# Node features loaded already turned, normalised by VectorE with scales read back from memory, edges normalised by ScalarE: a graph network layer on one Trainium2 core

## The reference, cut to what matters

```python
h = relu(layernorm(x))                          # x: 50000 x 128, no gain or bias
rel_inputs = concat([h[src], h[dst], edge_attr], -1)       # 25000 edges, receivers = dst
rel_effects = relu(rel_inputs @ re_w1 + re_b1) @ re_w2 + re_b2     # hidden width 256, out 128
agg_effects = segment_sum(rel_effects, receivers, 50000)
out = x + relu(concat([h, agg_effects], -1) @ ea_w1 + ea_b1) @ ea_w2 + ea_b2
```

## Time and profile before

| | |
|---|---|
| median of three runs | 955.74 us |
| profiled execution | 956.01 us, of it span 954.1 us |
| PE busy | 97% of the span |
| DVE, ACT, POOL busy | 78%, 63%, 64% |
| mean granted TensorE clock | 0.987 of full speed |
| moved by DMA | 151.88 MB, mean 159 GB/s |

### The profile page before, as it was taken

The page is one execution under the profiler, slowest core; times in us unless marked ns, Lnnn a source line. Parts: engine busy times, 40 slices in busy tenths (PEclk is TensorE's granted clock), DMA queues, the critical chain, the costliest instruction groups (busy, mean ns, idle before and its releaser), DMA issues.

```text
span 954.1 us, 21049 instructions
## 1 busy us (share of the span) xinstructions
PE 923.3 (97%) x6450; PEld 817.8 (86%) x6450; DVE 740.1 (78%) x2155; ACT 605.5 (63%) x1180; POOL 609.1 (64%) x600
## 2 busy tenths in 40 slices
PE   4879999999999999999999999999999999999987
PEld 4668998898898899889889889988988988998876
DVE  5887788788788878878877887886887788788562
ACT  1447666666666766666666676666666667666653
POOL 7785776776677677677667767767766776772320
PEclk7979999999999999999999999999999999999999
DMA  6253655555565565555556556555555655554442
GB/s 200 75 148 113 183 163 168 150 177 175 151 186 168 151 183 163 168 151 176 172 155 185 167 153 183 162 169 158 169 174 151 186 167 152 169 177 146 124 123 76
DMA packets 114105, 151.88 MB, mean 159 GB/s; under 512 B 17984, under 2 KB 70080, under 8 KB 113984
## 3 DMA queue, kind: packets, MB, share of 16 engines
q1 hardware_dynamic: 101440, 124.73, 43.2%
q0 software_dynamic: 12544, 25.72, 10.2%
HBM read 104.92 MB, written 45.46 MB: 158 GB/s over the span
## 4 chain that ended last, share of the span: by engine, by line
PE 94%; DVE 3%; SPq 1%; issue 1%; ACT 1%; DMA 0%; DVEq 0%
PE l_ps L531 33%; PE l_ps L546 27%; PE l_ps L536 17%; PE agg_ps L496 7%; PE edge_ps L479 4%; PE node_ps L487 4%; PE node_ps L471 1%; SPq L294 0%; DVE rel_row L831 0%; DVE hot L844 0%; SPq L300 0%; DVE lo L804 0%; DVE h L797 0%; DMA drow_i<-in_dst_rows 0%; DMA win<-rel_rows 0%
## 5 line engine op out<-in xcount | busy, mean ns | idle before, releaser
L386 POOL DMA_INDIRECT gath<-in_x,dst_all x196 | 200.2, 1022 | 59.7 <-issue 59.7
L386 POOL DMA_INDIRECT gath<-in_x,src_all x196 | 195.0, 995 | 52.9 <-issue 51.7
L546 PE MATMUL l_ps<-w2n,hid 128*128 128x128 f32 x1568 | 193.6, 277 | 0.0
L655 ACT ACTIVATE hid<-l_ps,b1n 128x512 f32<-128x512 f32 x196 | 135.0, 689 | 82.4 <-PE l_ps L536 82.4
L409 POOL TENSOR_TENSOR ea_lo<-ea_in,ea_hi 128x512 fp32r<-128x512 f32 x45 | 74.3, 1651 | 171.6 <-ACT ea_hi L629 171.6
L546 PEld LDWEIGHTS l_ps<-w2n,hid 128*128 128x128 f32 x1568 | 182.9, 192 | 0.1
L810 DVE SCALAR_TENSOR_TENSOR lo<-node_ps,hi 128x512 fp32r<-128x512 f32 x98 | 67.3, 687 | 146.1 <-ACT hi L638 146.1
L663 ACT ACTIVATE h<-xin,shift,rs 128x128 f32<-128x128 f32 x392 | 165.2, 486 | 0.0
L531 PE MATMUL l_ps<-hi,w1n_hi 128*128 128x512 f32 x392 | 155.7, 397 | 0.4 <-ACT hid L655 0.4
L531 PE MATMUL l_ps<-hi,w1n_lo 128*128 128x512 f32 x392 | 155.4, 396 | 0.0
L402 POOL TENSOR_TENSOR xb<-xin,b2n 128x512 f32<-128x512 f32 x98 | 131.0, 1354 | 33.5 <-DVE res L838 33.5
(11 more groups left out here) (98 smaller groups left out, 1566.1 us busy)
## 6 DMA issues: line engine op xcount, KB each, us to landing
win<-rel_rows SPq DMA_DIRECT2D x392, 98.0 KB
xin<-in_x_tiles SPq DMA_DIRECT2D x98, 256.0 KB, 4.2
out<-res SPq DMA_DIRECT2D x98, 256.0 KB, 3.4
rel_rows<-rel_row SPq DMA_DIRECT2D x49, 392.0 KB, 2.4
ea_in<-in_ea_t SPq DMA_DIRECT2D x49, 256.0 KB, 3.2
gath<-in_x,src_all POOLq DMA_INDIRECT x196, 2.7
gath<-in_x,dst_all POOLq DMA_INDIRECT x196, 2.9
w1e<-in_L_gnn_re_w SPq DMA_DIRECT2D x1, 384.0 KB, 3.6
```

The source lines that it names most:

```text
L386: nc.gpsimd.indirect_dma_start(gath[b][:, s, k, :], None, x, bass.IndirectOffsetOnAxis(ap=idx[:, e * T + k:e * T + k + 1], axis=0)).then_i ...
L546: last = nc.tensor.matmul(l2_ps[turn % 2][:, k * P:(k + 1) * P], hid[r][:, c, k * P:(k + 1) * P], w[:, c, :], start=(c == 0), stop=(c == C ...
L655: nc.scalar.activation(hid[r][:, c, :], l1_ps[c][:, :], ACT.Relu, bias=b[:, c:c + 1]).then_inc(hid_set, 1)
```

## The change

The host hands over a second copy of x with features on partitions (`x_t`), and SP loads from it a 128 x 512 piece for each node tile (`load_xt`). `turn_nodes` and `node_ps` go; the freed bank gives each tile of a pair its own `agg_ps`. Statistics still come from `xin`. As nodes now lie along the free dimension, the scale and shift of each node are needed on all partitions: DVE writes them to `norm`, SP stores them to memory (`keep_norm`, 8 KB), waits for that, and loads them back to every partition (`load_norm`, 1 MB), a pair ahead of their use. DVE applies them with four operations of 128x512 a pair (`normalise_pair`), the high and low parts of features are taken from SBUF, and edges of joint steps are normalised by ACT in four portions between its `hidden` operations. The orders of all engines are rewritten: on SP the loads of `x_t` stand ahead of the windows; on POOL `keep_x` stands ahead of the gathers; on DVE `mark(2)` and all lows of features stand ahead of `edge_results`. `edge_step` keeps its edge normalisation on DVE.

```diff
+            def load_xt(r, j):
+                wait(sp, normed[r], j - 1)
+                sp.dma_start(xt[r][j % 2][:, :], columns(x_t, tile_no(r, j))).then_inc(xt_loaded[r][j % 2], 16)
+            def keep_norm(j, fast):
+                sp.wait_ge(shift_set, stats_turn(j, fast) + 1)
+                wait(sp, norm_loaded[j % 2], 16 * (j // 2))
+                sp.dma_start(node_norm[j % 2, :].rearrange("(p f) -> p f", p=P),
+                             norm[j % 2][:, 1, :, :].rearrange("p v f -> p (v f)")).then_inc(norm_kept, 16)
+            def load_norm(j):
+                sp.wait_ge(norm_kept, 16 * (j + 1))
+                for r in (1, 2):
+                    wait(sp, normed[r], j - 1)
+                sp.dma_start(spread_norm[j % 2][:, :, :, :, :].rearrange("p n v r k -> p (n v r k)"),
+                             node_norm[j % 2:j % 2 + 1, :].to_broadcast([P, P * ST])).then_inc(norm_loaded[j % 2], 16)
...
             def joint_step(e, j):                      (SP)
-                for r in (1, 2):
-                    if j + 1 < NJ:
-                        load_window(r, j + 1)
+                ahead = pair_of(e + 1)
+                for r in (1, 2):
+                    load_xt(r, j + 1)
+                for r in (1, 2):
+                    load_window(r, j + 1)
                 if e + 2 < EG:
                     load_ea(e + 2)
+                keep_norm(ahead, True)
                 if j > 0:
                     store(2, j - 1, True)
+                load_norm(ahead)
...
                 store_rel(e, True)
                 store(1, j, True)
...
             def joint_step(e, j):                      (POOL)
+                for r in (1, 2):
+                    keep_x(r, j + 1, True)
                 set_dst(e)
                 if e + 2 < EG:
                     gather(e + 2)
                 if e + 1 < EG:
                     low_ea(e + 1)
...
             def joint_step(e, j):                      (PE)
                 for r, n in ((0, e), (1, j), (2, j)):
                     for c in range(C):
                         layer1(r, n, turn + r, c)
-                if j + 1 < NJ:
-                    turn_nodes(1, j + 1)
-                    sum_window(1, j + 1)
+                sum_window(1, j + 1)
                 if e + 1 < EG:
                     turn_edges(e + 1)
                 layer2(0, turn)
                 layer2(1, turn + 1)
-                if j + 1 < NJ:
-                    turn_nodes(2, j + 1)
-                    sum_window(2, j + 1)
+                sum_window(2, j + 1)
                 layer2(2, turn + 2)
...
             def joint_step(e, j):                      (ACT)
                 if more:
-                    normalise(1, j + 1, True)
+                    high_ea(e + 1, True)
                 hidden(0, turn, 0, before_edge(e, True))
...
                 hidden(0, turn, 1, before_edge(e, True))
                 if more:
+                    normalise_edges(e + 1, range(0, 1))
                 hidden(1, turn + 1, 0, before_node(1, j, True))
+                if more:
+                    normalise_edges(e + 1, range(1, 2))
                 hidden(1, turn + 1, 1, before_node(1, j, True))
...
+                high_features(1, j + 1, True)
+                high_features(2, j + 1, True)
+                high_sums(1, j + 1, True)
                 if more:
                     high_edges(e + 1)
                 edge_highs(e, True)
                 edge_mids(e)
+                high_sums(2, j + 1, True)
...
+            def scale_nodes(r, j):
+                dve.wait_ge(norm_loaded[j % 2], 16 * (j // 2 + 1))
+                dve.wait_ge(xt_loaded[r][j % 2], 16 * (j // 2 + 1))
+                wait(dve, node_lo_set, tile_no(r, j - 1) + 1 if j > 0 else 0)
+                nc.vector.tensor_tensor(tiled(h[r]), tiled(xt[r][j % 2]), norm_of(0, r, j), ALU.mult).then_inc(scaled[r], 1)
+            def shift_nodes(r, j):
+                dve.wait_ge(scaled[r], j + 1)
+                nc.vector.tensor_tensor(tiled(h[r]), tiled(h[r]), norm_of(1, r, j), ALU.add).then_inc(normed[r], 1)
...
             def joint_step(e, j):                      (DVE)
...
                 if j > 0:
                     node_results(2, j - 1, True)
                 invert(*what)
-                if e + 1 < EG:
-                    normalise_edges(e + 1, range(T))
-                if more:
-                    mark(1, j + 1)
-                    low_nodes(1, j + 1)
+                mark(1, j + 1)
+                normalise_pair(j + 1)
+                mark(2, j + 1)
+                low_features(1, j + 1)
+                low_features(2, j + 1)
+                low_sums(1, j + 1)
                 if e + 1 < EG:
                     low_edges(e + 1)
                 edge_results(e, True)
-                if more:
-                    mark(2, j + 1)
                 edge_rests(e)
                 node_results(1, j, True)
                 edge_lows(e)
-                if more:
-                    low_nodes(2, j + 1)
+                low_sums(2, j + 1)
```

More of the change, by code:

```diff
@@ L99, in gnn_program @@
         rest = sb("rest", [P, T, D])
-        tiles = [2 * T, T, T]
         parts = [2, 2, 2]
-        h = [sb(f"h{r}", [P, tiles[r], D]) for r in range(3)]
+        h = [sb("h0", [P, 2 * T, D]), sb("h1", [P, G]), sb("h2", [P, G])]
         st = sb("st", [P, ST, 6])
@@ L110, in gnn_program @@
         sd = sb("sd", [P, ST])
-        rs = [sb(f"rs{b}", [P, ST]) for b in range(2)]
-        shift = [sb(f"shift{b}", [P, ST]) for b in range(2)]
+        norm = [sb(f"norm{b}", [P, 2, 2, 2 * T]) for b in range(2)]
+        spread_norm = [sb(f"spread_norm{b}", [P, P, 2, 2, T]) for b in range(2)]
         hi = [sb(f"hi{r}", [P, parts[r], G], F32R) for r in range(3)]
@@ L119, in gnn_program @@
         xb = [None] + [[sb(f"xb{r}{b}", [P, T, D]) for b in range(2)] for r in (1, 2)]
+        xt = [None] + [[sb(f"xt{r}{b}", [P, G]) for b in range(2)] for r in (1, 2)]
         win = [None] + [sb(f"win{r}", [P, T, ROW]) for r in (1, 2)]
@@ L161, in gnn_program @@
         normed = [sem(f"normed{r}") for r in range(3)]
+        norm_kept = sem("norm_kept")
+        norm_loaded = [sem(f"norm_loaded{b}") for b in range(2)]
+        scaled = [None] + [sem(f"scaled{r}") for r in (1, 2)]
         edges_turned = sem("edges_turned")
@@ L455, in joint_step @@
                     low_ea(e + 1)
-                if j + 1 < NJ:
-                    for r in (1, 2):
-                        keep_x(r, j + 1, True)
             def pair_step(j, fast):
@@ L578, in enter @@
                 pe.wait_ge(loaded[1], LOADS)
-                for r in (1, 2):
-                    turn_nodes(r, 0)
-                    (sum_window if fast else sum_windows)(r, 0)
+                if not fast:
+                    for r in (1, 2):
+                        sum_windows(r, 0)
             def joint_step(e, j):
```

212 lines of the change are left out of this document (114 added, 98 removed).

## The result

| | before | after |
|---|---|---|
| median | 955.92 us (954.33 to 956.46) | 1120.97 us (1116.97 to 1124.07) |
| ratio | | 1.173 (95%: 1.170 to 1.176) |
| span of the profiled execution | 954.1 us | 1122.3 us |
| first and last store of edge results in the joint steps | 86.20, 910.97 us | 93.09, 1073.89 us |
| mean step, store to store (45) | 18.33 us | 21.80 us |

The changed kernel is 17% slower. Slower was forecast; the predicted 1053 us was 68 us too low, and the time lies 6 us above the range (1022 to 1115).

The account below looks back on a forecast made before the run. PE's work was taken to bound the kernel at 18.34 us a step; the change closes a 20.5 us loop through SP. 45 x (20.5 - 18.34) = +97, beginning -1.5, tail +2: span 1051.6, time 1053 us, range 1022 to 1115.

Parts of the forecast that it names:

- the loop through SP: Joint step: edge store, second tile's window loads, landing, `mark(2)`, `edge_results`, `edge_lows`, store; 20.5 us against 18.34; chance 0.70.
- The rival that PE stays the bound: Second tile's windows on SP land within 10.3 us of the store, all turning is won: 916 us; chance 0.09.
- The 40 us of turnings: PE's turning matmuls (line 487) go, 40 us over the span, leaving PE a step of 17.45 us.
- the beginning: Before the first joint step: loses two turnings and some order, about -1.5 us.
- the tail: After the joint steps: two of the three pair steps each carry the new SP issues, +2 us.
- The lock: Rival: `keep_x(1)` on POOL holds DVE's `edge_lows` for 0.6 to 1.2 us; 1107 to 1121 with half rate; chance 0.15.
- The node operations: DVE's four 128x512 scale and shift operations a step, 0.69 us each, next starting after 0.61: 2.4 us a step.
- the near row: Strided reads of scales and shifts on DVE cost 0.2 us an operation, 0.8 in all, covered; taken as nothing.
- The cover of 1.3 us: DVE free at 12.1 us after the store, windows land at 13.4; norm arithmetic free unless dearer than 0.9 us each.
- The landing: From SP's last window issue to data and semaphore for the mark: 1.8 us; extra bytes may add 0 to 0.5.
- The clock: Rival: gaps in PE's step make its granted clock fall in each step: 1150 us; chance 0.04.
- POOL's loop: `keep_x` ahead of gathers, waiting for `node_results(2)`: 1.3, 10.6 for eight gathers, 2.4 landing: 14.3 us, inside 20.5 less statistics.

Follow-up runs that it names:

- the experiment meant for it: Changed kernel with scales read from adjacent elements, plus POOL's gathers ahead of both `keep_x`: 1123.61 us, ratio 1.177.
- the fastest reordered kernel: Changed kernel, DVE, SP and POOL reordered, each portion of ACT's edge normalisation moved behind the `hidden` operation it stood ahead of: 1025.40 us, ratio 1.075.
- the first reordered kernel: Changed kernel with turned features behind x, `mark(1)` behind node operations, `mark(2)` behind `edge_results`, POOL's order `low_ea`, gathers, `keep_x` twice: 1076.27 us, ratio 1.122.
- the second: As the first reordered kernel, but POOL's order is gathers, `low_ea`, `keep_x` twice: 1098.17 us, ratio 1.149.

## Why the prediction was right or wrong

**What bounds the kernel, and the direction.** PE's work stopped being the bound, and the loop through SP took over: shown by the kernel before with only its mark moved (+31 us), by the chain, and by the measured terms, of which SP's to the last issue (11.56 against 11.6) and DVE's from the mark to `edge_results` (3.63 against 3.62) came out. What was wrong is a rival that belonged into the sum and terms that were too small. The rival that PE stays the bound fell: it needed the second tile's windows within 10.3 us of the store, and they were issued, not yet landed, at 11.56. The 40 us of turnings were taken from PE, but its busy time in the joint steps did not fall: 18.33 us a step before, 18.62 after (18.5 in the steps at full granted clock), where I had 17.45 left. The share of 0.85 that I had forecast (17.45 of 20.5) came out as 18.62 of 21.80, which is luck.

**Where the 71 us of span beyond the forecast went.** The joint steps took 980.8 us against 922, +59; the beginning +8.4 (93.09 instead of 86.20 less 1.5); the tail +3.3 (48.4 after the last store, forecast 45.1).

**The lock was a rival and should have been a term.** Of the 59 us, 45 x 0.88 = 40 are the stretch from `edge_results` to `edge_lows`. I gave this rival 0.15, with `keep_x(1)` as the only partner and 0.6 to 1.2 us as the price. The step of the prediction that failed is that choice of partner, and with it the term put at nothing. What I read for `keep_x(1)`, that DVE is first by 0.05 us, held in 37 of the 49 edge tiles, where `edge_lows` took its 0.69; but I did not place `low_ea`, which the new order puts last on POOL. With `keep_x(2)` from 5.2 us after the store (515.67 in the trace after), 1.3 for it and my own 10.6 for the gathers it starts at 17.1 and ends at 18.4, when `edge_results` was forecast for 17.0 and `edge_rests` for 18.4: by my own numbers they just meet, and the slower gathers push `low_ea` into `edge_rests` and `edge_lows`. Alone it holds `edge_rests` by up to 1.4 us; where `keep_x(1)` follows it with no gap, the two hold a DVE operation for up to 2.6 us beyond its 0.69 (3.25 in all) instead of one for 1.2. That the measured time lies at the top of this rival's 1107 to 1121 is luck: those figures don't follow from its terms, since 20.5 with 0.6 to 1.2 is 21.1 to 21.7, and with 1.1 more 22.2 to 22.8. The Trainium skill (SBUF — State Buffer, Who interferes with whom) calls the shared port pair an exclusive lock; the trace agrees, with 2.60 us instead of 0.69 and with 0.75 in the mean again once POOL's order is changed.

**The node operations were mis-sized.** 1.05 us in the mean instead of 0.69. I took the near row, a stride of 24 bytes over 16 elements, and it was no guide for 64 bytes over 512. The cover of 1.3 us was used up almost to the end: the last one ends at 13.55, the mark starts at 13.82. In 22 of the 45 steps the mark followed them without a wait, so in half of the steps the cover was gone. It isn't shown that they cost the loop anything there: with adjacent numbers they end 1.3 us earlier and the mark comes no sooner. What I did not ask is what they do to POOL: beside them a gather takes 1.70 us in the mean and 14 take 2.6 us or more, and that made `low_ea` late. The Trainium skill (SBUF — State Buffer, Door 1: The DMA port swizzle) has a penalty for each access that moves to another 16-byte line; I said the rows showed hardly any of it. At this stride the runs do show it: 1.05 against 0.70 with the numbers adjacent.

**The landing was mis-sized.** From last issue to mark 2.3 us in the mean (forecast 1.8): +0.43 on `mark(2)`, 45 x 0.43 = 19 us. In the steps in which the mark waited it is 2.26 as well. I had allowed 0 to 0.5 for the extra bytes and taken none. The read-back explains 0.1 of it at most; that gathers now run beside the second tile's windows is a difference that the traces show, but whether it is the cause stays open, as the experiment meant for it did not move them.

**The beginning.** I had it 1.5 us shorter. VectorE, then GpSimd:

```profile
59.19 4.82 DVE L891 TENSOR_TENSOR rel_row<-rest,rel_row 128x512 bf16<-128x512 f32 x1
...
86.60 1.29 DVE L870 SCALAR_TENSOR_TENSOR lo<-h,hi 128x512 fp32r<-128x512 f32 x2 [3.42 <-ACT hi L683]
```

```profile
58.47 4.98 POOL L460 TENSOR_TENSOR xb<-xin,b2n 128x512 f32<-128x512 f32 x4
```

Four `keep_x` in a row hold one `edge_lows` for 4.82 us; later DVE waits for ACT's high parts, in a stretch where PE was granted half its clock (67 to 84 us).

**The clock.** This rival did not come as a cost: PE is busy 0.85 in the joint steps at a mean granted clock of 0.97, with 13 falls to 0.50 of some 3 to 7 us each, and the 15 steps touched by one last 21.76 us against 21.81 of the others. Columns as in the earlier trace rows:

```profile
93.09:1073.89 980.80, 837.73 (x5478) 699.30 (x5477) 810.25 (x1746) 537.41 (x1069) 612.33 (x524) 0.97 0.67 212
```

**POOL's loop.** I had checked it at 14.3 us plus statistics and called it covered. It was, for this kernel (DVE waits 2.2 us for gathers in all), but narrowly, since a gather lands in 4.6 to 5.1 us and not in 2.4: with the mark 0.67 us earlier, waits for gathers and `low_ea` took part of it back. By these waits, that is why single edits paid less than forecast.

## What to carry to other kernels

When work is taken from the engine that bounds, write down every closed loop through the other engines and DMA queues with its length, not the longest alone: here PE's own work was 18.3 us a step, the loop through SP 19.0 in the kernel before with one mark moved and 21.8 in the changed one, one through ACT 19.0 in the fastest reordered kernel, and one through POOL close behind, and a single reordering in DVE's list was enough to close the first. Where VectorE reads two SBUF operands on such a loop, place every GpSimd operation of the new order in time as well, see which of them follow each other without a gap, and count the full length of such a row. A price read at one stride doesn't carry to another, and an operation that is covered on its own engine may still slow its neighbour.

## What the runs showed of the hardware

- A 128x512 fp32 VectorE operation whose second operand is read with a stride of 64 bytes took 1.05 us, 0.70 with it adjacent.
- Beside the strided operations the issue of an indirect gather took 1.70 us in the mean, nine times 3.57 or more (once 5.38), instead of 0.94; beside adjacent ones 1.01 in the mean and 1.46 at most.
- GpSimd operations back to back did not let a waiting VectorE operation in between: it was held for two of them (2.60 us) and for four (4.82).
- The recorded starts did not tell alone who is held: `keep_x`, 0.05 us behind `edge_lows` (once 0.35), was held itself in 37 cases (mostly 1.8 us), while `low_ea`, 0.28 to 0.30 us behind `edge_rests`, held that in 6 (2.13). No run shows why, and starts on GpSimd are rough.
- A 392 KB store landed in 8.7 us behind 2 MB of loads issued on the same queue (one step of the first reordered kernel; median 7.6 in the second), 2.4 in the kernel before.
